# A wait for the last but one between the placing writes of edge rows, and a drain at the end of each block

## What is computed

```python
h = relu(layernorm(x)); x = x + L0(h, edge_attr_64, src, dst, edge_type)   # attention weighted, by relation
h = relu(layernorm(x)); x = x + L1(h)      # two sums over neighbours
h = relu(layernorm(x)); x = x + L2(h)      # four graph convolutions, each one sum over neighbours
h = relu(layernorm(x)); x = x + L3(h, edge_attr_48)
# L3: sums = segment_sum(edge_attr_48, src), cnt = segment_sum(1, src)
#     comb = concat(x, sums / max(cnt, 1), u); three dense layers
```

## Time and profile before

| | us |
|---|---|
| median of 3 timed runs | 4683.87 (4682.92 to 4687.05) |
| span of the profiled execution | 6104.5 |
| POOL busy in it | 3187.4 |
| PE busy in it | 3504.6 |
| DVE busy in it | 2563.8 |
| first gather starts | 202.8 |
| last placing write starts | 5840.8 |

### The profile page before, as it was taken

The page is one execution under the profiler, slowest core; times in us unless marked ns, Lnnn a source line. Parts: engine busy times, 40 slices in busy tenths (PEclk is TensorE's granted clock), DMA queues, the critical chain, the costliest instruction groups (busy, mean ns, idle before and its releaser), DMA issues.

```text
span 6104.5 us, 83728 instructions
## 1 busy us (share of the span) xinstructions
PE 3504.6 (57%) x18191; PEld 1755.8 (29%) x18192; DVE 2563.8 (42%) x7891; ACT 1503.7 (25%) x3741; POOL 3187.4 (52%) x3191
## 2 busy tenths in 40 slices
PE   5377777777777777776324544345365345455347
PEld 2133333333333333333101222112132112222136
DVE  6266666666666666666330020131120021120368
ACT  3133333323323232322211111111111112111158
POOL 2455555555555555555376555645625635626720
PEclk8588888878888887888656676667666667667679
DMA  5333333333333333333123444334324334324256
GB/s 181 93 77 81 81 78 78 77 80 77 77 77 80 77 77 78 80 77 71 38 93 135 145 146 131 119 112 145 107 79 144 111 132 146 108 79 156 79 200 237
DMA packets 593641, 646.86 MB, mean 106 GB/s; under 512 B 423668, under 2 KB 430418, under 8 KB 587261
## 3 DMA queue, kind: packets, MB, share of 16 engines
q1 hardware_dynamic: 374705, 459.40, 23.2%
q0 software_dynamic: 101760, 110.75, 9.2%
q10 hardware_dynamic: 117068, 75.50, 4.1%
HBM read 451.74 MB, written 190.23 MB: 105 GB/s over the span
## 4 chain that ended last, share of the span: by engine, by line
PE 35%; issue 21%; another core or an unknown queue 21%; DVE 10%; DMA 8%; ACT 2%; POOL 2%; DVEq 1%; SPq 0%; ACTq 0%; POOLq 0%
PE bank L1742 10%; PE bank L1743 7%; PE bank L1823 6%; PE bank L1747 6%; DMA ld_all<-adjacency 3%; DMA rel_table<-ld_all 2%; DMA rel_and_z<-adjacency 1%; DVE hid_T L1305 1%; DMA ld_all<-l_sorted 1%; POOL l_sorted L711 1%; DVE hid_T L1326 1%; DVE hid_T L1584 1%; PE bank L1939 1%; PE bank L1771 1%
## 5 line engine op out<-in xcount | busy, mean ns | idle before, releaser
L711 POOL DMA_INDIRECT l_sorted<-arena,l_pos x1504 | 1539.2, 1023 | 1339.3 <-ACT arena L854 877.4
L686 POOL DMA_INDIRECT ld_all<-rel_table,rel_and_z x1564 | 1545.8, 988 | 1133.0 <-remote 503.2
L1742 PE MATMUL bank<-hid_T 128*128 128x400 f16 x2346 | 965.7, 412 | 672.6 <-issue 539.8
L1743 PE MATMUL bank<-hid_T 128*128 128x384 f16 x2346 | 940.5, 401 | 44.3 <-issue 43.5
L1326 DVE TENSOR_SCALAR hid_T<-count_key,hid_T 128x400 f16<-128x400 int16 x2346 | 592.1, 322 | 754.5 <-remote 526.7
L1823 PE MATMUL bank<-rel_and_z,ld_all 128*128 128x512 fp8e4 (+1 forms) x1872 | 522.3, 414 | 602.9 <-issue 534.1
L1823 PE MATMUL bank<-ld_all 128*128 128x512 fp8e4 (+1 forms) x1950 | 511.4, 420 | 337.4 <-issue 138.4
L1747 PE MATMUL bank<-ld_all,arena 128*32 x4692 | 527.1, 250 | 123.3 <-issue 121.3
L1742 PEld LDWEIGHTS bank<-hid_T 128*128 x2346 | 255.9, 109 | 1157.3 <-issue 1153.9
L774 ACT CAST ld_all<-bank 128x400 fp8e4<-128x400 f32 x391 | 191.1, 489 | 1551.6 <-remote 999.7
L1266 DVE COPY accT<-bank 128x512 f32<-128x512 f32 (+1 forms) x78 | 51.1, 656 | 1215.4 <-remote 797.1
(11 more groups left out here) (289 smaller groups left out, 4103.0 us busy)
## 6 DMA issues: line engine op xcount, KB each, us to landing
ld_all<-adjacency SPq DMA_DIRECT2D x72, 1600.0 KB
rel_and_z<-adjacency SPq DMA_DIRECT2D x72, 1600.0 KB
l_sorted<-zeros SPq DMA_DIRECT2D x147, 424.0 KB
arena<-in_edge_attr SPq DMA_DIRECT2D x195, 256.0 KB
ld_all<-l_sorted SPq DMA_DIRECT2D x33, 1277.5 KB, 6.0
adjacency<-ld_all ACTq DMA_DIRECT2D x391, 100.0 KB
rel_table<-ld_all SPq DMA_DIRECT2D x49, 520.0 KB, 3.6
ld_all<-rel_table,rel_and_z POOLq DMA_INDIRECT x1564
```

Source lines behind the costliest of these rows:

```text
L686: pool.indirect_dma_start(ring[:, c % RING, 0:TW], None, rel_table, bass.IndirectOffsetOnAxis(ap=rel_i[:, c:c + 1], axis=0)).then_inc(s(f" ...
L711: pool.indirect_dma_start(l3_sorted, bass.IndirectOffsetOnAxis(ap=l3_pos[0:parts, n * SB_K + k:n * SB_K + k + 1], axis=0), rows16[q][0:par ...
L1742: pe.matmul(b0[:, 0:w0], low[:, 0:P], pair_hot[q % 2][:, k, 0:w0], start=k == 0, stop=k == CG - 1)
L1743: pe.matmul(b1[:, 0:GW - w0], low[:, P:2 * P], pair_hot[q % 2][:, k, 0:GW - w0], start=k == 0, stop=k == CG - 1)
```

## The change

It does three things. GpSimd counts the landings of the writes by two semaphores, `l3_placed0` and `l3_placed1`, for the even and the odd writes of a block, and before write k (k from 2 on) it waits until write k - 2 has landed; at the end of each block it waits for both, and adds one to a new semaphore, `l3_drained`. ScalarE (L843) and SyncE (L587) wait for `l3_drained` where they waited for `l3_moved{q}`. And the three index loads share one semaphore, so that each cast waits for all three. The two early blocks keep their semaphores.

```diff
-                sp.dma_start(at[:, 0:ET - 1, :], ...).then_inc(s(f"idx_loaded{n}"), 16)
+                sp.dma_start(at[:, 0:ET - 1, :], ...).then_inc(s("idx_loaded"), 16)
...
-                for q in range(3):
-                    sp.wait_ge(s(f"l3_moved{q}"), 16 * SB_K * (len(range(q, NSB + 1 - EARLY, 3)) + (q < EARLY)))
+                for block in range(EARLY):
+                    sp.wait_ge(s(f"l3_moved{block}"), 16 * SB_K)
+                sp.wait_ge(s("l3_drained"), NSB + 1 - EARLY)
...
                     for k in range(SB_K):
+                        if k > 1:
+                            pool.wait_ge(s(f"l3_placed{k % 2}"), 16 * (m * SB_K // 2 + k // 2))
                         pool.indirect_dma_start(l3_sorted, bass.IndirectOffsetOnAxis(ap=l3_pos[0:parts, n * SB_K + k:n * SB_K + k + 1], axis=0),
-                                                rows16[q][0:parts, k, :], None).then_inc(s(f"l3_moved{q}"), 16)
+                                                rows16[q][0:parts, k, :], None).then_inc(s(f"l3_placed{k % 2}"), 16)
+                    for odd in range(2):
+                        pool.wait_ge(s(f"l3_placed{odd}"), 16 * (m + 1) * SB_K // 2)
+                    pool.sem_inc(s("l3_drained"), 1)
...
                 if m >= 3:
-                    act.wait_ge(s(f"l3_moved{m % 3}"), 16 * SB_K * (m // 3 + (m % 3 < EARLY)))
+                    act.wait_ge(s("l3_drained"), m - 2)
...
-                v.wait_ge(s(f"idx_loaded{n}"), 48)
+                v.wait_ge(s("idx_loaded"), 3 * 48)
```

More of the change, by code:

```diff
@@ L381, in _ @@
                 rest = FULL - (ET - 1) * P
-                sp.dma_start(at[:, 0:ET - 1, :], a[0:whole].rearrange("(t c p) -> c t p", c=P, p=P)).then_inc(s(f"idx_loaded{n}"), 16)
-                sp.dma_start(at[0:rest, ET - 1, :], a[whole:FULL * P].rearrange("(c p) -> c p", p=P)).then_inc(s(f"idx_loaded{n}"), 16)
-                sp.dma_start(at[rest:rest + 1, ET - 1, 0:TAIL], a[FULL * P:E].rearrange("(c p) -> c p", p=TAIL)).then_inc(s(f"idx_loaded{n}"), 16)
+                sp.dma_start(at[:, 0:ET - 1, :], a[0:whole].rearrange("(t c p) -> c t p", c=P, p=P)).then_inc(s("idx_loaded"), 16)
+                sp.dma_start(at[0:rest, ET - 1, :], a[whole:FULL * P].rearrange("(c p) -> c p", p=P)).then_inc(s("idx_loaded"), 16)
+                sp.dma_start(at[rest:rest + 1, ET - 1, 0:TAIL], a[FULL * P:E].rearrange("(c p) -> c p", p=TAIL)).then_inc(s("idx_loaded"), 16)
             sp.dma_start(l3_pos[:, 0:NSB * SB_K].rearrange("p (s k) -> p s k", k=SB_K),
```

## The result

The changed kernel takes 5402.14 us (median; 5391.63 to 5408.98), the kernel before 4683.4 us beside it: a ratio of 1.1534 [1.1517, 1.155], 719 us slower. The forecast was 5242 us, +558 us.

What follows compares the result with a forecast made beforehand. GpSimd's queue was taken as the bound (sum 4652 us). Full blocks 570 us, slow writes -20 us and the last block +8 us gave +558 us: 4683.87 + 558 = 5242 us, range 4880 to 5750 us, chance 0.82.

Steps and rivals of the forecast that it cites:

- The bound: Whole kernel: GpSimd's queue bounds the timed runs nearly from first gather to last write, sum 4652 us against 4683.87 us.
- the cover is real: Placing writes: GpSimd already waits for ScalarE in timed runs, 17 us per block, hiding new waits; 4684 us, chance 0.05.
- The waits between the writes: Full blocks of placing writes: a pair takes T = 3.24 us against 2.54 us before, with two writes in flight.
- the waits cost only the drains: Placing writes: landing and release fit in 2.54 us, so each block costs +1.9 us; +87 us, 4770 us, chance 0.04.
- Landing under load: Placing writes beside loads land late: +2040 us if all take 4.43 us, 5920 us part way; chance 0.06.
- The drains: End of each full block: 1.27 us second write, 2.43 us drain and 0.81 us next block's start, 4.51 us together.
- The slow writes and the last block: Placing writes: slow ones hide partly in the new waits, -20 us; the last block takes 85 against 87, +8 us.
- faster: Placing writes: two in flight remove 82 us of slow writes, landing at most 1.7 us; -27 us, 4657 us, chance 0.03.
- the index semaphore and the count's hop: First index cast waits 0 to 3.3 us more, taken as 0; ScalarE's and SyncE's hop some 0.1 us, taken as nothing.
- What the profile was to show: Placing writes: gaps alternate 0.30 and 1.0 us, landing waits several hundred us, block starts 3.2 us; span grows 50 to 550 us.

## Why the prediction was right, and where it was off

**The bound: right.** The sum of what GpSimd needs gave 4652 us and said that its queue bounds the timed runs; the second trace of the kernel before shows it directly, with 24.6 us of waits in 1504 writes. The rival "the cover is real" fell with it. The loss of the stretch (723 us) is the loss of the kernel (719 us).

**The waits between the writes: the right queue and the right wait, but both parts of the term wrong.** The forecast had T = 2.43 + 0.81 = 3.24 us for each pair, 0.70 us over 2.54, or 15 x 0.70 x 46 = 483 us. The measured excess inside blocks is 651 us, 0.94 us for each pair on the mean, T = 3.48. But both parts of the term were wrong, and they erred in opposite directions. By its own last line (wrong "if landings take other than 2.4 us, if the release takes other than 0.8 us") the working failed here, whatever the sum. The release is 0.27 us and not 0.81; the row that I took it from is that of a write released by ScalarE at the start of a block, and at the start of a block it is still right (0.89). I had named 0.30 as the other bound and chose wrongly. With it and a quiet landing of 2.2 to 2.3 us, T would have been 2.5, which hides: of 1380 waits 1086 cost nothing. This alone is the rival "the waits cost only the drains", 4770 us, and it holds in quiet stretches. The landing beside loads is 4.6 to 8.0 us and not 2.43: I took the gathers' landing, measured in a quiet stretch at the start of the kernel, for writes that run beside 1600 KB loads. The average share of the DMA engines, on which I argued against that, hides that they are busy for 0.85 in some stretches and 0.10 in others. "Landing under load", with a chance of 0.06 and every write as slow, was too much of it; its mechanism holds for most of the 194 waits over 1 us, and the drains-only rival for the rest. That the sum came near is luck: the two errors partly cancel. With the release put right alone, T = 2.43 + 0.27 = 2.70 us would have given less than the lower end of the forecast.

The Trainium skill (DMA: Bandwidth & Descriptors, section Anatomy of one DMA — SWDGE (gpsimd) path) gave an estimate of 2.1 us for one write; the trace agrees in quiet, with 2.2 us. The same page (Latency and other measured facts) has an HBM latency of 2 us in place of 0.2 us at high load, which would make an estimate of about 4 us for a write; the rows show a rise in the same direction, but to 4.6 to 8.0 us for 115 of the 145 writes at a DMA share of 0.6 or more, and the measurement decides.

Two small slips in the working change nothing in the sum. In "Landing under load", T = 4.2 us makes a block of 68.5 us and +1280 us, not +1240 us. And the 33 packets of a write include the last block's: a full write has (49664 - 2560) / 1472 = 32.

**The drains: near.** The forecast had 4.51 - 2.54 = 1.97 us for each of 46 ends, 91 us; measured are 82 us. Alone they cost 157 us, of which the late starts of every 112th write are a part. No term of the forecast stands for those (25 us in the changed kernel).

**The slow writes and the last block.** -20 us were taken for slow writes, and -7 us are seen (131 against 138). They also fall out of the rival "faster": outside the last block the kernel before has 49 writes of over 1 us, the changed one 52 and the one with one in flight 44, so they don't come from too many in flight. All but one of these 145 stand where the DMA share is under 0.6; what slows them was not tried. The last block took 69 us from its first write to the end of its last, against 62 before: +7 us for the forecast's +8, though the forecast had 85 and 87. The 87 came from the stretched trace; the 85 took 5.24 us for a pair, where the chain of the changed kernel has landings of 3.8 to 4.3 us and 0.29 us of release. The reason that the forecast gave for that block's late landing, few engines that share a write, was read from the mean busy share (14.9% of 16), which does not say how many engines carry one write; what the runs show is that with 128 rows to a write the lateness is gone (2.27 us).

**Nothing for the index semaphore and the count's hop: right.** The first is a measured 0.9999. The second adds nothing at the end: from the last landing to the next load it is 0.13 us with the count, and 5845.36 - 5845.20 = 0.16 us before. In the chain of the changed kernel the last write's landing, the count and the load behind it are

```profile
5132.97 4.42 DMA l_sorted<-arena,l_pos
5137.39 0.04 POOLq L718
5137.43 0.02 issue
5137.44 0.03 SPq L588
5137.47 0.05 issue
5137.52 6.23 DMA ld_all<-l_sorted
```

**What the profile was to show.** The wait for GpSimd's own landings is there and is 1086.8 us, not "several hundred"; the gap does not alternate between 0.30 and 1.0 us but is 0.30 in quiet and up to 5.8 us inside a block. The first write of a block follows the last one by 3.1 to 3.4 us in 40 of 46 cases, near the forecast's 3.2, and by 5.8 to 7.1 us in the other six, one of them beside loads (3286.07 to 3293.06). And the profiled span did not grow by 50 to 550 us: it fell from 6104.5 to 5401.0, since the first trace of the kernel before was itself the odd one. Its 1452 us over the sum were no property of the kernel; the second trace, at 4679.5 us, is 27 us over it.

**What stays open.** Whether a write is late because its packets stand behind those of the loads in the DMA engines, or because the memory answers late, no run here tells: each run took loads away or left them. In the kernel without adjacency loads, 12 of the 64 longer waits inside blocks (21 us) have neither an edge load next to them nor the place of a 112th write; what they wait for was not followed up. Why every 112th write starts late in some kernels and not in others, and why the first trace was stretched, is not known either.

## What to carry to other kernels

A wait on one's own DMA a few issues back is free as long as the landing takes less than the time to issue those between, and that landing has to be read beside the heaviest traffic that the queue meets, not in a quiet stretch nor by an average of the DMA share: here 2.2 us became 5 to 8. Two in flight without drains cost 629 us, four in flight some 200 inside the blocks, eight nothing that can be seen; 47 drains alone cost 157 us. When a profiled span is 30% over the timed median, profile the same kernel again before taking waits from it.

## What the runs showed of the hardware

- Without waits, indirect writes of 128 rows of 292 bytes are issued by GpSimd with 0.30 us between them whatever the load of the DMA engines (all five bins), while their landing, where a wait shows it, goes from 2.2 us to 4.6 to 8.0 us.
- A write with 106 rows takes GpSimd 1.55 us and lands after 4.4 us; one with 128 rows takes 0.97 us and lands after 2.2 us in quiet. Filling it up made the kernel 0.44% faster (0.9956).
- In the changed kernel and in the one with drains alone, the 114th placing write and every 112th after it start 0.4 to 7.0 us late with no releaser shown (25 and 37 us in all); the kernel before and the one with eight in flight have none of this.
- A wait that is already met costs GpSimd nothing that can be seen (the kernel with eight in flight: 24 waits in a block, 6 us in the whole stretch), and one that is not is followed by the next start 0.27 us after the landing.
